# A routed expert layer in units of 32 tokens: rows gathered eight units ahead instead of four, landings awaited later, four output buffers, and the plan moved up

## The reference

```python
# x (8, 100, 512), ctx_1024 (8, 722, 512); router_w (512, 16)
# w1 (16, 512, 1024), b1 (16, 1024), w2 (16, 1024, 512), b2 (16, 512)
n = layernorm(x)
x1 = einsum('eth,efh->etf', n, ctx); x2 = x1          # the same context twice
x = x + einsum('etf,efh->eth', gelu_tanh(x1) * x2, ctx)
n = layernorm(x)
logits = n @ router_w; assign = argmax(logits); w = sigmoid(logits[assign])
hh = gelu(n @ w1[assign] + b1[assign])                # exact gelu
out = x + w * (hh @ w2[assign] + b2[assign])
```

## Time and profile before

| | |
|---|---|
| median of three runs | 386.09 us |
| the profiled execution | 381.66 us, span 379.6 us |
| granted TensorE clock, mean | 0.887 of 2.4 GHz |
| busy: PE, DVE, ACT, POOL | 267.8, 137.6, 39.8, 103.3 us |
| chain that ended last | gathers into `grow` 33% of the span, issue 14%, GpSimd 8% |
| moved | 99.46 MB, mean 262 GB/s |

### The profile page before, as it was taken

The page is one execution under the profiler, slowest core; times in us unless marked ns, Lnnn a source line. Parts: engine busy times, 40 slices in busy tenths (PEclk is TensorE's granted clock), DMA queues, the critical chain, the costliest instruction groups (busy, mean ns, idle before and its releaser), DMA issues.

```text
span 379.6 us, 12189 instructions
## 1 busy us (share of the span) xinstructions
PE 267.8 (71%) x5032; PEld 228.2 (60%) x5032; DVE 137.6 (36%) x534; ACT 39.8 (10%) x107; POOL 103.3 (27%) x157
## 2 busy tenths in 40 slices
PE   0999989999997956855649456767575667577610
PEld 0868856876693856745548355667474667467510
DVE  3016434644443751532233333222233143525410
ACT  1201111111110200010000000000000001101000
POOL 1002102211114122422234323322232134435451
PEclk9999999999999979896798987688779669989975
DMA  7989999999999992099940999999908940000000
GB/s 267 329 279 299 270 330 342 377 362 347 377 386 412 416 403 82 16 360 416 416 183 11 355 414 418 413 364 377 404 13 321 417 194 16 22 17 23 20 7 6
DMA packets 19704, 99.46 MB, mean 262 GB/s; under 512 B 4072, under 2 KB 4528, under 8 KB 11348
## 3 DMA queue, kind: packets, MB, share of 16 engines
q1 hardware_dynamic: 16852, 93.91, 65.8%
q0 software_dynamic: 2816, 5.03, 4.0%
HBM read 96.33 MB, written 3.82 MB: 264 GB/s over the span
## 4 chain that ended last, share of the span: by engine, by line
DMA 33%; issue 14%; POOL 8%; POOLq 2%
DMA grow<-rows,idx 33%; POOL out L833 6%; POOL idx L842 2%; POOLq L842 0%; POOLq L837 0%; POOL grow L845 0%; POOLq L908 0%; POOLq L858 0%; POOLq L855 0%; POOLq L850 0%; POOLq L844 0%; POOLq L838 0%; POOLq L859 0%; POOLq L851 0%; POOLq L857 0%
## 5 line engine op out<-in xcount | busy, mean ns | idle before, releaser
L403 PE MATMUL bank<-W_early,unit 128*32 128x128 f32 x1600 | 63.9, 326 | 55.6 <-issue 55.5
L403 PEld LDWEIGHTS bank<-W_early,unit 128*32 128x32 f32 x1600 | 56.2, 132 | 61.0 <-issue 60.9
L381 PE MATMUL bank<-W_early,xT 128*32 128x128 f32 x1600 | 58.6, 305 | 11.6 <-DVE xT L696 7.8
L721 DVE SCALAR_TENSOR_TENSOR unit<-bank,grow,res 128x128 f32 (+1 forms) x32 | 11.2, 350 | 140.4 <-POOLq L838 129.5
L381 PEld LDWEIGHTS bank<-W_early,xT 128*32 128x32 f32 x1600 | 52.7, 125 | 15.3 <-DVE xT L696 8.9
L833 POOL DMA_INDIRECT out<-unit,at x28 | 29.1, 1040 | 116.5 <-issue 116.5
L316 PE MATMUL bank<-xnT,area 128*128 128x100 f32 (+1 forms) x384 | 51.7, 290 | 0.6 <-ACT xnT L484 0.6
L316 PEld LDWEIGHTS bank<-xnT,area 128*128 128x128 f32 (+1 forms) x384 | 48.7, 202 | 4.4 <-issue 3.5
L328 PE MATMUL bank<-area,hidT 128*100 128x512 f32 (+1 forms) x96 | 44.7, 604 | 1.8 <-DMA area<-in_ctx_rest 1.6
L501 ACT ACTIVATE unit<-unit 128x128 f32<-128x128 f32 x64 | 19.7, 310 | 215.8 <-DVE unit L703 215.7
L845 POOL DMA_INDIRECT grow<-rows,idx x32 | 35.3, 1102 | 25.6 <-POOL idx L842 24.9
(11 more groups left out here) (89 smaller groups left out, 201.1 us busy)
## 6 DMA issues: line engine op xcount, KB each, us to landing
W_early<-in_w SPq DMA_DIRECT2D x52, 1024.0 KB, 11.8
area<-in_w SPq DMA_DIRECT2D x12, 1024.0 KB, 10.9
area<-in_ctxT_a SPq DMA_DIRECT2D x8, 768.0 KB, 10.6
area<-in_ctx_main SPq DMA_DIRECT2D x8, 768.0 KB
area<-in_ctxT_b SPq DMA_DIRECT2D x8, 676.0 KB, 11.0
area<-in_ctx_main SPq DMA_DIRECT2D x8, 512.0 KB
rows<-xw POOLq DMA_DIRECT2D x8, 206.2 KB, 7.3
first_area<-in_x SPq DMA_DIRECT2D x8, 192.0 KB
```

What stands on the lines that cost most here:

```text
L381: last = nc.tensor.matmul(p_hh[half][U * q:U * q + U, :], xT[:, U * k:U * k + U], w[:, q, KH * half:KH * half + KH], start=(k == 0), stop= ...
L403: last = nc.tensor.matmul(p_y[U * q:U * q + U, 0:P], hT[:, c, :], W2[slot][:, c, P * q:P * q + P], start=(c == 0), stop=(c == KF - 1), til ...
L721: nc.vector.scalar_tensor_tensor(out=y[:, bass.ds(to, P)], in0=p_y[:, 0:P], scalar=row_of(j)(P + 3, 1), in1=res[:, :], op0=ALU.mult, op1=A ...
```

## The change

- `grow` has eight slots, and there are eight landing semaphores. A gather is issued eight units ahead instead of four; GpSimd's loop is unrolled over eight steps, with up to seven more in nested branches.
- In a step the landing that is awaited stands last and is that of gather i + 5, issued three steps earlier.
- `y` has four buffers, in `first_area`, and `s_yfree` starts at 4 instead of 2. `tok_all` moves from `area` to `first_area`, `idx` has four buffers.
- At the start of the ring four gathers are issued before the first is awaited, then one gather per landing. The wait for the last batch's written rows moves behind the first two outputs.
- `early_slots` and `early_table` stand near the start of the last batch, and the four early gathers before `put_rows` of the batch before it.
- `plan_ends` stands ahead of `finish(0, 2)`, `token_weights` and `plan_units` follow one unit earlier, `tokens` is in two parts (seven batches, then one), and `all_slots` stands ahead of unit 3's second layer.
- Unit 1's second layer is split in two halves with the last ranks between them. ScalarE runs a one-column `Gelu` on a blank tile ahead of the first unit, and its first copy waits for the zeroing.

```diff
-        grow = sb("grow", [P, EARLY, ROW])
+        grow = sb("grow", [P, RING, ROW])
...
-        y = unit[:, 6 * KH * U:8 * KH * U]
         tok_e = unit[0:T, 0:EB * P].rearrange("p (b q) -> p b q", b=EB)
-        tok_all = area[0:T, 2 * WL:2 * WL + NB * P].rearrange("p (b q) -> p b q", b=NB)
+        y = first_area[:, D:D + Q * P]
+        tok_all = first_area[0:T, XR * D - NB * P + D:XR * D + D].rearrange("p (b q) -> p b q", b=NB)
...
                 hidden(b, 0)
+                if b == FIX + 2:
+                    early_slots()
                 if b > 0:
                     transpose_x2(b - 1)
...
-            second_layer(1, 0)
+            second_half(1, 0, 0)
             ranks(NB - 1)
+            second_half(1, 0, 1)
...
             residual(3)
+            all_slots()
             second_layer(3, 2)
             first_layer(4, 3, 0)
             first_layer(4, 3, 1)
             residual(4)
-            all_slots()
             second_layer(4, 3)
...
+            nc.scalar.activation(blank[:, :], blank[:, :], ACT.Gelu)
             copy_rows(x2T, p_t, s_x2ps, s_x2T, NB - 1)
...
+                if b == FIX + 2:
+                    early_table()
                 multiply(b, 0)
...
+            dve.wait_ge(s_xnps, NB)
+            tokens(0, NB - 1)
             add_x2(NB - 1)
...
             write_gate(NB - 1)
+            plan_ends()
+            tokens(NB - 1, 1)

             finish(0, 2)
...
-            plan_ends()
             token_weights()
-            tokens()
+            plan_units()

             finish(1, 3)
...
-            plan_units()
+            unit_table()

             finish(2, 4)
...
             def take(i, r):

-                nc.gpsimd.tensor_copy(idx[r % 2][:, :], lin[:, bass.ds(i, 1)]).then_inc(s_idx, 1)
+                to = (r + EARLY) % RING
+                nc.gpsimd.tensor_copy(idx[r % Q][:, :], lin[:, bass.ds(i, 1)]).then_inc(s_idx, 1)
                 pool.wait_ge(s_idx, number(i + 1))
                 pool.sem_inc(s_apart_p, 1)
-                nc.gpsimd.indirect_dma_start(grow[:, r, :], None, rows_q,
-                                             bass.IndirectOffsetOnAxis(ap=idx[r % 2][:, :], axis=0),
+                nc.gpsimd.indirect_dma_start(grow[:, to, :], None, rows_q,
+                                             bass.IndirectOffsetOnAxis(ap=idx[r % Q][:, :], axis=0),
                                              bounds_check=bound_piece, oob_is_err=False).then_inc(s_g[r], 16)

             def landed(i, r):
-                pool.wait_ge(s_g[r], number(4 * i + (16 - 4 * r)))
+                pool.wait_ge(s_g[r], number(2 * i + (16 - 2 * r)))
                 pool.sem_inc(s_rows, 1)

             def step(i, r):

                 nc.gpsimd.tensor_copy(at[r % 2][:, :], lin[:, bass.ds(i, 1)]).then_inc(s_at, 1)
-                landed(i + (Q - 1), (r - 1) % Q)
                 pool.wait_ge(s_at, pool.snap(i + 1))
                 pool.wait_ge(s_yo, pool.snap(i + (EARLY + 2)))
                 pool.sem_inc(s_apart_p, 1)
-                put_out(i + EARLY, r, at[r % 2][:, :])
-                take(i + EARLY, r)
...
-            pool.sem_inc(s_yfree, 2)
+                put_out(i + EARLY, r % Q, at[r % 2][:, :])
+                take(i + RING, r)
+                landed(i + (RING - 3), (r + RING - 3) % RING)
+
+            pool.sem_inc(s_yfree, 4)
...
             put_rows(NB - 1)
-            rows_landed(pool, NB - 1)
             pool.wait_ge(s_yo, 2)
             put_out(0, 0, tab_e[:, 0:1])
             pool.wait_ge(s_yo, 3)
             put_out(1, 1, tab_e[:, 1:2])
+            rows_landed(pool, NB - 1)
             pool.wait_ge(s_lin, 1)
-            take(0, 0)
-            take(1, 1)
-            landed(0, 0)
-            early_step(2)
-            early_step(3)
+            for i in range(Q):
+                take(i, i)
+            for i in range(2):
+                landed(i, i)
+                take(Q + i, Q + i)
+            for j in range(2, EARLY):
+                pool.wait_ge(s_yo, j + 2)
+                put_out(j, j, tab_e[:, j:j + 1])
+                landed(j, j)
+                take(Q + j, Q + j)
+            landed(Q, Q)
```

83 lines of the change are left out of this document (41 added, 42 removed).

## The result

The changed kernel took **321.13 us** (median of 4 runs, 318.38 to 322.61), beside 383.6 for the kernel before in the same runs: a ratio of 0.8435, interval 0.8331 to 0.8538. The forecast was 299 with a range of 287 to 318, so the direction was right and the time lies 3 us outside. The profiled execution took 322.61 us on a span of 320.5.

What follows compares the result with a forecast made beforehand. The ring output, gather, landing, output bounds the kernel at 7.45 us a unit. After the change GpSimd starts at 156.8, takes 22.7 steps of 4.82 and 4.3 of 4.2 to 284.3, plus 10.74: span 295.0, scaled 299 us, range 287 to 318.

Steps and rivals of the forecast that it cites:

- The ring cut: GpSimd's ring: gather landings awaited three steps after issue, `finish` up to three outputs ahead, ending the 7.45 us a unit.
- GpSimd's own step, 4.2: GpSimd's loop: output, gather, two copies and the ways between them take 4.2 us a unit, none of it removed.
- The wait that stays, 4.82: GpSimd's loop: the wait for the previous output's landing, 6.4 us under load, makes a step 4.82 us.
- GpSimd is later and decides: End of the loop: GpSimd could start output 31 at 284.3, TensorE at 276.5, so GpSimd sets the time.
- rival 4: Output's landing stays below 5.1 us, no wait binds and TensorE decides: 287 to 292 us, chance 0.12.
- TensorE with VectorE, 4.40 within an expert and 4.75 at a change: Loop units: 15 expert changes in 28 give 4.59 us a unit on TensorE, at 2.4 GHz.
- Weights: Weight loads in the loop: 10.0 us an expert at 418 GB/s, load lasting until about 266 us.
- Rival 5: Slower than before: GpSimd's wait behind `put_out` binds again where doubled traffic queues; 394 us, chance 0.02.
- Rival 3: Weights bind in the loop, slots free late or the rate below 418 GB/s: 297 to 303 us, chance 0.10.
- Rival 2: TensorE's granted clock stays low in the loop: 327 us at 0.76, 302 at 0.9; chance 0.10.
- The start: Start of the ring: `lin` at 136.4, the loop's first unit at 145.5, output 4 near 156.8 instead of 167.82.
- The end: End of the loop: output 31 starts at 284.3, with 10.74 us behind it, for a span of 295.0.

Runs made afterwards that it cites:

- narrow second layer: Seven of the second layer's eight chunks multiplied with 32 of each 128 columns, on the changed kernel without later weight loads and with `hidden` first: 284.0 us.
- chip D: The changed kernel run again unchanged, in a group of kernels on another chip: 302.5 us, ratio 0.7766 to 0.7863 to before, quiet step 4.20 us.
- chip A: The changed kernel in the result's own runs, on a chip the record doesn't number: 321.1 us, ratio 0.8331 to 0.8538 to before, quiet step 5.07 us.
- older output: Changed kernel, but GpSimd awaits the output two back before an output, not the one before behind it: 322.7 us; again, 320.8 beside the change's 320.4.
- without the stream: Changed kernel without loading the weights of experts 5 to 15, the first five experts' being used again: 305.2 us, and 281.1 on the chip of the 302.5.
- B: Chip of the first follow-up group, where the changed kernel without later weight loads took 305.2 us, quiet step 5.08; the change itself was not run there.

## Why the prediction was wrong, by its steps

- **The ring cut.** Right. Gathers left the chain, and putting the wait back gave 373.8 where 7.45 a step makes 369.
- **GpSimd's own step, 4.2.** Right in size: 4.15 to 4.20 where nothing else binds (narrow second layer, and the change on chip D, where 19 of 28 outputs follow GpSimd's own copy). **The wait that stays, 4.82, and with it "GpSimd is later and decides"**: failed at the long step. On chip A 22 outputs wait for `finish`, and the older output gives nothing. The landing itself was forecast well: 5.5 to 7.1 us under load on D, 2.3 at the end, for 6.4 and 2.3, and at the short step the wait took part. What happened on A is rival 4's mechanism, TensorE decides, at a price that rival put 32 us too low.
- **TensorE with VectorE, 4.40 within an expert and 4.75 at a change: the step of the forecast that failed.** The pair in the earlier trace rows gave nearly the right length in two of six groups: on D it is 4.20 within and 4.55 at a change. In the other four it is 5.07 at both. Over 27 steps that is (5.07 - 4.59) x 27 = 13 us in the term; between groups it measured 302.5 against 319.4 to 321.1, 17 to 19 us. Why TensorE takes the longer step is open. Nothing in the trace of before shows it: TensorE there waited for the ring in each unit, its semaphores don't lag, and the kernel before takes 382 to 385 everywhere.
- **The missing term.** TensorE's code has none in the sum. Seven stretches of 1.0 to 2.5 us, 12.6 in all, lie in the profiled run; without the stream the kernel is some 18 us faster by the ratios, at either step. The sum has 123.9 us for the 27 steps from `finish` 4 to `finish` 31. They took 154.5 on A and 140.2 on B without the stream, 135.9 on D and 119.4 there without it. So the stream is 14 to 17 us and the longer step 19 to 21, and where neither is, on D without the stream, the term holds within 5 us. By TensorE's own term output 31 could start at 276.5; it started at 308.9, 32.4 later. Against the 284.3 of the forecast, where GpSimd had already filled 7.8 of this, it is 24.6.
- **Weights.** 411 to 415 GB/s in the loaded stretches for the 418 taken, and no stretch over 0.9 us of TensorE ends at a piece's landing. The last unit of expert 3 is the eighth of the loop (2 + 1 + 1 + 4), not the ninth; that moves the loaded part by one step and the sum by less than 1 us. Rival 5's sum gives 392, not 394. The Trainium skill (DMA: Bandwidth & Descriptors, Where 436 GB/s comes from) has a share of about 358 GB/s binding there; this trace shows more, and the measurement decides. Rival 3 named the right victim, TensorE idle under load, with the wrong cause: its 301 comes by weights' landings, where the code does it.
- **The clock.** Rival 2's 302 to 327 holds the time, but its mechanism doesn't: the granted clock is 1.00 in the loop on A, with half of it in three stretches of 3.4 us only (at 144.9, 175.6 and 254.1). The second and third begin 1.1 and 1.7 us behind the end of a code stretch, so a code stretch can cost more than its own length, by an estimate up to 1.7 us (half of 3.4). Without the stream, on B, there is none between 129 and 292 us.
- **The start.** Right, with luck in it. `lin` starts at 134.7 (136.4 forecast), the loop's first unit at 144.81 (145.5), output 4 at 155.4 (156.8). The tail behind output 31 is 11.6 for 10.74. But with the same code up to there `lin` starts between 129.3 and 141.0 in the profiles of these experiments, so an agreement within 2 us is chance as much as skill.
- **The end.** Output 31 at 308.9 instead of 284.3 on A, at 284.2 on D. On D the forecast's number is met with the wrong split: a step of 4.86 made of 4.20 to 4.55 and of waits for code, from an output 4 at 153.0 instead of 156.8. That is luck.

## What to carry to other kernels

When a wait is cut out of a ring, the next bound has never been seen running: the trace of before shows its parts only with pauses between them, and a pause hides a slow part and a late refill alike. Give such a term an upper bound from its slowest neighbour, not the one pair that suits. Code is traffic too: an unrolled body for each expert costs about a packet each, and while the queues were full of weights seven of 13 packets cost TensorE 1 to 2.5 us. And where two kernels differ by a few per cent, compare them on one chip: the same program stood at 302.5 and 320.4 us on two, with the kernel before within 1% on both. Last, an idle stretch can be told by its place: one that stands at the same record of the program in every run is the program's, one at the edge of a piece is that piece's.

## What the runs showed of the hardware

- TensorE stood idle until 2.30 to 2.58 us after a 16 KB packet on the instruction queue had started, 24 times in three profiles, while the weights streamed, and at the same records of the program. In the three profiles without the stream it stood idle for over 0.75 us once, in front of a layer. The profile puts the change's 27 packets at 0.6% of the queues' time.
- Limiting the weights to two pieces in flight cut a piece's landing from 12.2 to 5.7 us and the rate from about 415 to 355 GB/s, and left those stretches. Waits for weights ended 0.13 us behind the last record of the landing.
- The same program takes 0.88 us more per quiet unit in four groups of six, at a granted clock of 1.00 and with like records; the semaphore behind the layer shows it.
- A step of GpSimd with two indirect DMAs and two one-column copies takes 4.15 to 4.20 us where nothing else holds it.
